# Row maxima in spare PSUM columns, and weighted values scaled before their halves are added

## What is computed

```
x = x + 0.5 * ffn(layernorm(x))
x = x + attention(layernorm(x))
x = x + 0.5 * ffn(layernorm(x))

ffn(x)       = (silu(x @ Wu.T) * (x @ Wg.T)) @ Wd.T        # hidden 1024, weights made ternary
attention(x) = softmax(rope(q) @ rope(k).T / sqrt(16) + causal) @ v @ wo   # 16 heads of 16
```

## Time and profile before

| | |
|---|---|
| median of 3 runs | 969.17 us (969.09 to 969.97) |
| span of the profiled execution, first to last instruction | 966.7 us |
| its time around the span, by the median | about 2.5 us |
| PE busy | 791.4 us, 82% |
| DVE busy | 742.8 us, 77% |
| ACT busy | 637.3 us, 66% |
| POOL busy | 552.8 us, 57% |
| mean granted TensorE clock | 0.930 |

### The profile page before, as it was taken

The page is one execution under the profiler, slowest core; times in us unless marked ns, Lnnn a source line. Parts: engine busy times, 40 slices in busy tenths (PEclk is TensorE's granted clock), DMA queues, the critical chain, the costliest instruction groups (busy, mean ns, idle before and its releaser), DMA issues.

```text
span 966.7 us, 21146 instructions
## 1 busy us (share of the span) xinstructions
PE 791.4 (82%) x7488; PEld 601.0 (62%) x7488; DVE 742.8 (77%) x1640; ACT 637.3 (66%) x1349; POOL 552.8 (57%) x535
## 2 busy tenths in 40 slices
PE   1347879898987989888987989888999899878866
PEld 0235657676765767666765776666777767656544
DVE  3644577989895898869895898959888988867653
ACT  2113677877776787757776787857777778767542
POOL 1037565666664676746664675746676666644221
PEclk9959889999998999989998999989999999989687
DMA  8300000000000000000000000000000000000000
GB/s 304 95 1 1 1 1 1 2 13 1 13 1 4 12 2 12 2 14 1 13 1 4 12 2 12 3 14 1 13 1 13 1 13 2 12 1 13 1 12 12
DMA packets 9964, 15.30 MB, mean 16 GB/s; under 512 B 640, under 2 KB 9088, under 8 KB 9344
## 3 DMA queue, kind: packets, MB, share of 16 engines
q1 hardware_dynamic: 9280, 11.54, 3.5%
q10 hardware_dynamic: 576, 2.29, 0.6%
HBM read 9.63 MB, written 4.19 MB: 14 GB/s over the span
## 4 chain that ended last, share of the span: by engine, by line
issue 26%; POOL 21%; PE 21%; DVE 20%; ACT 10%; DMA 1%; POOLq 0%; DVEq 0%; SPq 0%; ACTq 0%
POOL hid_l L1032 5%; POOL prob_l L1025 4%; PE misc_ps L387 3%; POOL rope_s L1004 3%; PE up_ps L387 2%; PE down_ps L387 2%; PE misc_ps L499 2%; ACT prob L641 2%; POOL rope_c L1003 2%; PE probt_ps L452 2%; POOL rstd L982 2%; PE score_ps L406 2%; DVE neg_max L873 2%; PE pv_ps L434 2%; DVE silu_b L928 2%
## 5 line engine op out<-in xcount | busy, mean ns | idle before, releaser
L1032 POOL TENSOR_TENSOR hid_l<-hid,hid_h 128x512 f16<-128x512 f32 x128 | 148.7, 1162 | 267.0 <-ACT hid_h L656 259.3
L632 ACT ACTIVATE prob_h<-probt_ps 128x384 f16<-128x384 f32 x256 | 127.4, 498 | 118.0 <-PE probt_ps L452 116.0
L1025 POOL TENSOR_TENSOR prob_l<-prob_t,prob_h 128x384 f16<-128x384 f32 x128 | 117.9, 921 | 70.3 <-ACT prob_t L636 69.8
L641 ACT ACTIVATE prob<-score_ps,exp_bias,exp_scale 128x256 f32<-128x256 f32 x256 | 146.8, 573 | 1.8 <-DVE exp_bias L879 1.6
L452 PE MATMUL probt_ps<-ident_f,prob 128*128 128x128 f32 x768 | 135.0, 287 | 13.0 <-ACT prob_t L636 13.0
L387 PE MATMUL up_ps<-xt_hi,tern_up 128*128 128x256 f16 x512 | 129.2, 289 | 19.5 <-DVE tern_up L711 12.4
L387 PE MATMUL down_ps<-tern_down,hid_h 128*128 128x256 f16 x512 | 121.8, 277 | 19.5 <-POOL hid_l L1032 19.4
L387 PE MATMUL up_ps<-xt_lo,tern_up 128*128 128x256 f16 x512 | 129.2, 289 | 0.0
L873 DVE TENSOR_REDUCE neg_max<-score_ps 128x2 f32<-128x512 f32 x128 | 87.7, 685 | 53.3 <-PE score_ps L408 53.0
L387 PE MATMUL gate_ps<-xt_hi,tern_gate 128*128 128x256 f16 x512 | 125.9, 284 | 1.8 <-DVE tern_gate L711 1.8
L928 DVE SCALAR_TENSOR_TENSOR silu_b<-tanh_b,up_ps 128x512 f32<-128x512 f32 x128 | 87.2, 681 | 52.1 <-ACT tanh_b L650 52.0
(11 more groups left out here) (108 smaller groups left out, 1990.7 us busy)
## 6 DMA issues: line engine op xcount, KB each, us to landing
xs<-x SPq DMA_DIRECT2D x16, 256.0 KB, 2.8
out<-xs SPq DMA_DIRECT2D x16, 256.0 KB, 2.1
raw_gate<-w_gate_t ACTq DMA_DIRECT2D x1, 1024.0 KB, 7.5
raw_up<-w_up_t SPq DMA_DIRECT2D x1, 1024.0 KB, 7.7
raw_down<-w_down_t SPq DMA_DIRECT2D x1, 1024.0 KB, 10.4
raw_w<-wqkvo ACTq DMA_DIRECT2D x1, 1024.0 KB, 12.5
cos<-rope_cos SPq DMA_DIRECT2D x1, 512.0 KB, 13.7
sin<-rope_sin SPq DMA_DIRECT2D x1, 512.0 KB, 14.4
```

The costliest lines, as they stand in the source:

```text
L632: act.activation(prob_h[:, pair % 2, j, :], probt_ps[:, 0:384], ACT.Copy).then_inc(prob_h_done, 1)
L641: act.activation(prob[:, s % 2, j, 0:256], score_ps[:, j, 0:256], ACT.Exp, bias=exp_bias[:, j:j + 1], scale=exp_scale[:, :])
L1025: pool.tensor_tensor(prob_l[:, pair % 2, 0, :], prob_t[:, pair % 2, :], prob_h[:, pair % 2, 0, :], ALU.subtract).then_inc(prob_l_done[0], 1)
L1032: pool.tensor_tensor(hid_l[:, s % 2, :, :].rearrange("p m n -> p (m n)"), hid[:, s % 2, :], hid_h[:, s % 2, :, :].rearrange("p m n -> p (m ...
```

## The change

`neg_max` is no longer a tile in SBUF. It is the columns 384 to 387 of the first bank of `score_ps`, which the scores leave unused; `row_max` writes there and `exp_biases` reads there. Its output `exp_bias` stays in SBUF.

The last two operations on the product with v change places. `pv_scale` now comes first: it multiplies both halves, as they stand in PSUM, by the reciprocals, into a new SBUF tile `pv_norm` (128 columns). `pv_add` then adds the halves of `pv_norm` into `attn`. What frees `pv_ps` for PE's next product is now `pv_scale`. In every list the two names have changed places, so the extras ahead of the first and the second of the pair stay where they were.

```
-        neg_max = sb("neg_max", [P, 4])
-        pv_sum = sb("pv_sum", [P, NT, 2, HD])
+        pv_norm = sb("pv_norm", [P, NT * 2, 2, HD])
+        neg_max = score_ps[:, 0, 384:388]

-DVE_SLOT = ["row_max", "pv_inverse", "exp_biases", "pv_add", "misc_a", "pv_scale", "silu", "hidden",
+DVE_SLOT = ["row_max", "pv_inverse", "exp_biases", "pv_scale", "misc_a", "pv_add", "silu", "hidden",
             "prob_lo_1", "misc_b"]

-                pe.wait_ge(pv_sum_done, st.at(lambda t: SLOTS * (t - lag) + pair))
+                pe.wait_ge(pv_norm_done, st.at(lambda t: SLOTS * (t - lag) + pair))

-            def pv_add(st, s):
+            def pv_scale(st, s):
                 lag, pair = pv_parts(s)
                 if st.live(lag):
-                    dve.wait_ge(pv_done, st.at(lambda t: SLOTS * (t - lag) + pair + 1))
-                    dve.tensor_reduce(pv_sum[:, :, :, :].rearrange("p n j d -> p (n j) d"),
-                                      pv_ps[:, 0:4 * VW].rearrange("p (m w) -> p m w", w=VW)[:, :, 0:2 * HD]
-                                      .rearrange("p m (a d) -> p m d a", a=2), AX.X, ALU.add
-                                      ).then_inc(pv_sum_done, 1)
-
-            def pv_scale(st, s):
+                    dve.wait_ge(inv_done, st.at(lambda t: SLOTS * (t - lag) + pair + 1))
+                    dve.wait_ge(attn_done, st.at(lambda t: SLOTS * (t - lag) + pair))
+                    dve.tensor_tensor(pv_norm[:, :, :, :].rearrange("p m a d -> p m (a d)"),
+                                      pv_ps[:, 0:4 * VW].rearrange("p (m w) -> p m w", w=VW)[:, :, 0:2 * HD],
+                                      inv_sum[:, :, :, :].rearrange("p n j o -> p (n j) o")
+                                      .to_broadcast([P, NT * 2, 2 * HD]), ALU.mult).then_inc(pv_norm_done, 1)
+
+            def pv_add(st, s):
                 lag, pair = pv_parts(s)
                 if st.live(lag):
                     if pair == 0:
                         dve.wait_ge(attn_h_done, st.at(lambda t: t - lag))
-                    dve.wait_ge(inv_done, st.at(lambda t: SLOTS * (t - lag) + pair + 1))
-                    dve.wait_ge(pv_sum_done, st.at(lambda t: SLOTS * (t - lag) + pair + 1))
-                    dve.tensor_tensor(attn[:, :, 2 * pair * HD:2 * (pair + 1) * HD]
-                                      .rearrange("p n (j d) -> p n j d", j=2), pv_sum[:, :, :, :],
-                                      inv_sum[:, :, :, :].to_broadcast([P, NT, 2, HD]), ALU.mult
+                    dve.wait_ge(pv_norm_done, st.at(lambda t: SLOTS * (t - lag) + pair + 1))
+                    dve.tensor_reduce(attn[:, :, 2 * pair * HD:2 * (pair + 1) * HD]
+                                      .rearrange("p n (j d) -> p n j d", j=2),
+                                      pv_norm[:, :, :, :].rearrange("p (n j) a d -> p n j d a", n=NT), AX.X, ALU.add
                                       ).then_inc(attn_done, 1)
```

More of the change, by code:

```diff
@@ L88 @@
 }
-DVE_SLOT = ["row_max", "pv_inverse", "exp_biases", "pv_add", "misc_a", "pv_scale", "silu", "hidden",
+DVE_SLOT = ["row_max", "pv_inverse", "exp_biases", "pv_scale", "misc_a", "pv_add", "silu", "hidden",
             "prob_lo_1", "misc_b"]
 DVE_OTHER = {
-    1: ["pv_inverse", "row_max", "exp_biases", "pv_add", "misc_a", "pv_scale", "silu", "hidden", "prob_lo_1",
+    1: ["pv_inverse", "row_max", "exp_biases", "pv_scale", "misc_a", "pv_add", "silu", "hidden", "prob_lo_1",
         "misc_b"],
-    4: ["row_max", "pv_inverse", "exp_biases", "misc_a", "pv_add", "pv_scale", "silu", "hidden", "prob_lo_1",
+    4: ["row_max", "pv_inverse", "exp_biases", "misc_a", "pv_scale", "pv_add", "silu", "hidden", "prob_lo_1",
         "misc_b"],
@@ L97 @@
 DVE_EXTRA = {
-    (1, "pv_inverse"): ["ffn_added"], (2, "pv_scale"): ["rows_3"], (2, "prob_lo_1"): ["stats_3"],
+    (1, "pv_inverse"): ["ffn_added"], (2, "pv_add"): ["rows_3"], (2, "prob_lo_1"): ["stats_3"],
     (3, "row_max"): ["stats_wait_3"], (3, "pv_inverse"): ["mean_3"], (3, "exp_biases"): ["var_3"],
-    (3, "misc_a"): ["apply_3"], (5, "exp_biases"): ["ffn_added"], (5, "pv_add"): ["rows_1", "stats_1"],
-    (5, "pv_scale"): ["stats_wait_1"], (5, "silu"): ["mean_1", "var_1"], (6, "exp_biases"): ["rows_2"],
-    (6, "pv_add"): ["stats_2"], (6, "misc_a"): ["stats_wait_2"], (6, "pv_scale"): ["mean_2"],
+    (3, "misc_a"): ["apply_3"], (5, "exp_biases"): ["ffn_added"], (5, "pv_scale"): ["rows_1", "stats_1"],
+    (5, "pv_add"): ["stats_wait_1"], (5, "silu"): ["mean_1", "var_1"], (6, "exp_biases"): ["rows_2"],
+    (6, "pv_scale"): ["stats_2"], (6, "misc_a"): ["stats_wait_2"], (6, "pv_add"): ["mean_2"],
     (6, "silu"): ["var_2"],
@@ L320, in macaron_kernel @@
         prob_l_done = [sem("prob_l_done0"), sem("prob_l_done1")]
-        inv_done, pv_sum_done, attn_done = sem("inv_done"), sem("pv_sum_done"), sem("attn_done")
+        inv_done, pv_norm_done, attn_done = sem("inv_done"), sem("pv_norm_done"), sem("attn_done")
         attn_h_done = sem("attn_h_done")
```

## The result

The changed kernel takes 957.26 us in the median of four runs (952.9 to 959.47), the kernel before 969.57 in the same series (969.09 to 970.35): 12.3 us less, a ratio of 0.987 with an interval of 0.984 to 0.990. The forecast was 960.4. The profiled execution is the fastest of the four: its time is 952.9 us and its span 951.0. A difference of the two spans, 966.7 - 951.0 = 15.7 us, is therefore larger than that of the medians.

What follows compares the result with a forecast made beforehand. PE, the busiest engine, waits for DVE, whose instructions stall behind POOL's. Slot 5's -9.8 us and slot 3's +1.0 sum to -8.8, taking the median from 969.2 to 960.4 us; range 949.5 to 966.5.

Steps and rivals of the forecast that it cites:

- Slot 5: `var_s` ends with POOL's `k_row` instead of its `prob_l`: 0.82 us gained in each of 12 steps, -9.8 us.
- the stall only moves: Rival: `var_s` in slot 5 misses the handover and still waits for POOL's `prob_l`; 970.2 us, chance 0.13.
- Slot 6: `var_s` still held to the end of POOL's `prob_l`; gain under 0.1 us, taken as nothing.
- slot 6 gains too: Rival: `var_s` in slot 6 catches the handover ahead of `prob_l`, up to 0.75 us in 12 steps; 951.4 us, chance 0.17.
- Slot 3: `pv_add` on the path takes 0.28 us in place of 0.21: cost 0.07 us in 14 steps, +1.0 us.
- Slots 0, 1, 2, 4 and 7: DVE waits there for others, such as ACT's tanh or `prob_h`, so its savings bring nothing.
- Writes to PSUM: Row maxima written to PSUM: taken as no cost, bounded by 0.17 us for each reduction, 4.8 us at most.
- slower: Rival: writing row maxima to PSUM is dear; 979.2 us at 0.5 us each, chance 0.07.
- Row maxima that take longer than before: Listed sign that the prediction is wrong, about the reductions that now write to PSUM; no size given.
- The first step of the attention: Not in the sum; stalls in the first steps were allowed for in the own range's lower end, 957.
- PE's gap ahead of `product_v` in slot 6: Listed sign that the prediction is right: PE's idle time there near 0.4 us in place of 1.23.

Runs made afterwards that it cites:

- the maxima alone: Kernel before, with only the row maxima put in spare PSUM columns, sum first and scale second as before: 960.9 us, ratio 0.992.
- the other addition: Changed kernel, with the halves added by a tensor_tensor with two SBUF inputs in place of the reduction with one: 961.4 us, ratio 0.992.
- the scale alone: Kernel before, with only the scaling out of PSUM put ahead of the addition, row maxima left in SBUF: 961.1 us, ratio 0.991.
- POOL's order changed: Changed kernel, with POOL's rope addition put ahead of the power in slot 3 and nothing else: 942.4 us, ratio 0.972.
- `pv_add` last: Changed kernel, with `pv_add` of slot 3 moved from ahead of `silu` to behind `misc_b`: 951.1 us, ratio 0.979.

## Why the prediction was right

**Slot 5** carried the forecast: 0.82 us in 12 steps. Measured 0.87: `var_s` ended with `k_row`, and the two single-part runs show that this handover, and not the sum of the stalls removed, sets the gain. With both parts it held in all 12 steps; with the maxima alone and with the other addition, where `attn` is still of the kind that is stalled, it was lost in 2 and 3 of 12. The rival "the stall only moves" did not come in for the change, but it is no idle one. **Slot 6**: under 0.1 us was forecast, 0.14 measured; `var_s` lost its race by 0.08 us, so the rival "slot 6 gains too" did not come in, and in the changed kernel it is in slot 6 alone that the stall only moves. **Slot 3**: +0.07 forecast in 14 steps, +0.05 measured in 13, and gone in the runs where 64 columns stand in that place. **Slots 0, 1, 2, 4 and 7**: nothing forecast, and their medians agree to 0.01 us, but for the long slots 4. **Writes to PSUM**: 8 ns each, so 14 x 2 x 0.008 = 0.2 us in slot 3; the rival "slower" had needed 0.38 us each. Row maxima that take longer than before were listed as a sign of a wrong prediction; they did take longer, by too little to matter, and the sign should have had a size.

By the first pair of profiles the slots 3, 5 and 6 of the 12 steps together take 245.1 us before (81.1 + 86.5 + 77.5) and 233.3 after (81.8 + 75.7 + 75.8): -11.8, where the sum had -8.8 for all.

**What the sum left out.** The first step of the attention is not like the others: its eight slots take 46.4 us before and 42.6 after. I had put this in the range and not in the sum. The maxima alone give 43.0 and the scale alone 45.0, so most of it goes with `exp_bias`, whose stalls are 0.9 to 1.3 us there. But PE does not wait less in that step. Its row in the kernel before, and then in the changed one:

```profile
114.50:160.90 46.40, 39.67 (x359) 28.35 (x358) 36.13 (x82) 34.44 (x75) 29.10 (x28) 0.85 0.01 1
```

```profile
117.25:159.87 42.62, 36.07 (x358) 26.10 (x357) 30.13 (x82) 33.47 (x75) 29.03 (x28) 0.96 0.01 1
```

The columns are the stretch, its length, busy time and instructions of PE, PE's weight loads, DVE, ACT and POOL, then the granted clock. PE is idle for 6.7 and 6.6 us, and busy 3.6 us less with the same work, at a clock of 0.96 in place of 0.85. The gain of this step is thus one of the clock: it is at its lower level for 13.7 us of the step before, in both profiles of that kernel, and for 3.4 to 6.8 us in the three of the changed one. The runs with fewer stalls of `exp_bias` have less of it; by what way the one brings the other, no run tests. Against this gain stand the long slots 4, some 2 us more in this pair.

**Wrong in the list of signs**: PE's gap ahead of `product_v` in slot 6 is 0.80 us, and I had said 0.4. 0.4 came of 1.23 - 0.82, without PE's own earlier arrival. PE had been idle for 0.30 us earlier in slot 5, at the stacks' transposes, and that is gone: `q_stk` comes 0.43 us earlier, and so do the transposes. PE arrives sooner and waits longer, 1.23 + 0.43 - 0.87 = 0.79 us. The start of `product_v` is DVE's all the same.

**Open.** The profile's difference of spans, 966.7 - 951.0 = 15.7 us, has +2.8 ahead of the first `product_v`, -3.8 in the first step, -10.0 in the 12 steps and -4.7 behind them. The first and the last of these I can't put down to the change: in 14 profiles the first `product_v` starts between 114.5 and 117.4 us, in no order that goes with the kernels, and behind the 12 steps the second profile of the kernel before has 162.2 us in place of 165.1, within the 160.4 to 163.0 of the changed kernel's three. So the mechanism of the 12 steps is right, but that the total came within some 3 us of the forecast is partly luck: the sum did not have the first step, and the long slots 4 took some of it back.

The single parts were 4 us slower in the median than the changed kernel, and so was the kernel with the other addition. With the maxima alone and with the other addition slots 5 and 6 of the 12 steps are 3.0 and 4.6 us longer, by the lost handovers. With the scale alone they are not; its first step is 2.3 us longer than the changed kernel's, and the rest stays open.

## What to carry over

When two engines block each other over a port, ask of each blocked instruction which instruction of the other engine it waits for, and who is next: removing one stall lets the next instruction of that kind arrive earlier, at the same end of the same foreign instruction. The gain is the distance between two such ends, not the sum of the stalls. Here it came with the first fix, and grew again only when the last instruction of the kind moved away from POOL's work. Where another such instruction was left ahead of the last one, it had a race to win in every step, and lost it in 2 or 3 of 12, each time behind a long slot 4; the second fix brought no shorter slot, but kept all 12. So list all instructions of the kind in the stretch, ask for each which one the stall goes to next, and move or convert the last one as well.

## What the runs showed of the hardware

Slot 4 has two lengths, 5.11 and 6.2 to 6.3 us, with nothing between and the same instructions. The granted clock sets them apart. Two stretches of 5.6 us of the changed kernel, each from slot 4, the first with the short and the second with the long form:

```profile
438.00:443.60 5.60, 4.77 (x53) 3.81 (x54) 4.70 (x12) 5.46 (x13) 4.27 (x4) 1.00 0.01 3
489.00:494.60 5.60, 5.50 (x39) 3.88 (x38) 3.46 (x10) 4.33 (x10) 4.30 (x4) 0.76 0.01 3
```

The columns are as in the rows of the first step above. In the long form PE is busier with fewer instructions, and the clock is at its lower level, 1.2 GHz, for 3.4 us, which begin 0.1 us behind the slot's first `product_v` (488.20):

```profile
488.30:491.70 3.40, 3.40 (x27) 2.65 (x26) 2.08 (x7) 2.05 (x5) 2.46 (x3) 0.50 0.02 5
```

It follows slot 3, in which PE stood idle before the transposes of `xhat`. That wait in the changed kernel and with POOL's order changed:

```profile
436.24 0.66 PE L500 MATMUL misc_ps<-ident_f,xhat 128*128 128x128 f32 x4 [0.90 <-DVE xhat L825]
```

```profile
429.51 0.66 PE L500 MATMUL misc_ps<-ident_f,xhat 128*128 128x128 f32 x4 [0.44 <-DVE xhat L825]
```

With 0.90 us of idle time there, 2 to 7 of 12 steps had the long form, in 11 profiles of eight kernels; with 0.44 us none of 36 had, in three profiles of two kernels. PE's only other idle time in slot 3, ahead of the `product_v` that ends it, doesn't set them apart: it is 0.61 us in the changed kernel and with POOL's order changed, and 0.41 us with `pv_add` last, which had 7 long slots. So shortening a wait of PE by half a microsecond returned up to 1.2 us more in the slot behind it, and the four runs of POOL's order lie within 3.1 us of each other. What decides in which steps the clock falls is not shown. Whether the change itself draws more of them (2 and 3 before, 4, 6 and 7 after, but 2 and 4 with its parts) stays open.
